# Self attentions of a decoder: transposed scores from a second product block in place of turned probabilities

## The reference

```python
xn = (x - mu) / jnp.sqrt(var + 1e-06) * ln_g + ln_b
qkv = xn @ w_qkv.T + b_qkv
q, k, v = (qkv[0], qkv[1], qkv[2])
scores = jnp.einsum('bhqd,bhkd->bhqk', q, k) * scale
scores = jnp.where(causal[None, None], scores, -jnp.inf)
probs = jax.nn.softmax(scores / TEMP, axis=-1)
gate = jnp.clip(jax.nn.sigmoid(xn @ w_ent.T + b_ent), 0.1, 2.0)[:, None, None, :, 0]
out = jnp.einsum('bhqk,bhkd->bhqd', probs * gate, v)
return (out @ w_out.T + b_out) * 0.1
```

```python
att = att1 - lam * att2
y = jnp.einsum('bhts,bhse->bhte', att, v)
y = y * jax.lax.rsqrt(jnp.mean(y * y, axis=-1, keepdims=True) + RMS_EPS) * subln_w
y = y * (1.0 - LAMBDA_INIT)
return y.transpose(0, 2, 1, 3).reshape(B, T, 2 * C) @ c_w.T
```

## Time and profile before

| | us |
|---|---|
| median of 3 runs | 6188.18 |
| lowest and highest | 6187.22, 6196.38 |
| the profiled execution | 6208.25 |
| its span | 6206.5 |

### The profile page before, as it was taken

The page is one execution under the profiler, slowest core; times in us unless marked ns, Lnnn a source line. Parts: engine busy times, 40 slices in busy tenths (PEclk is TensorE's granted clock), DMA queues, the critical chain, the costliest instruction groups (busy, mean ns, idle before and its releaser), DMA issues. The chain is left out here.

```text
span 6206.5 us, 84643 instructions
## 1 busy us (share of the span) xinstructions
PE 4731.2 (76%) x22582; PEld 3354.9 (54%) x22582; DVE 3437.1 (55%) x5067; ACT 2441.8 (39%) x3674; POOL 1999.7 (32%) x1091
## 2 busy tenths in 40 slices
PE   7999999999798866669878888888486444432698
PEld 6778778888544755348845555555274222221344
DVE  3444444444345422444556666664646999987444
ACT  2345555555222311123335555554123555540122
POOL 0055555555100000000036666664001555550000
PEclk7789999999799965687779999998677666655699
DMA  2100000000011312121111112110020000000011
GB/s 74 48 8 16 16 16 16 16 16 8 13 42 29 70 36 58 41 82 31 28 43 43 42 42 46 43 38 20 11 43 20 22 21 21 21 16 0 5 46 38
DMA packets 153375, 193.27 MB, mean 31 GB/s; under 512 B 91760, under 2 KB 136576, under 8 KB 152864
## 3 DMA queue, kind: packets, MB, share of 16 engines
q1 hardware_dynamic: 152992, 188.87, 12.5%
HBM read 134.07 MB, written 19.05 MB: 25 GB/s over the span
## 5 line engine op out<-in xcount | busy, mean ns | idle before, releaser
L1021 POOL TENSOR_TENSOR pexp_lo<-arena,pexp_hi 128x800 fp32r<-128x800 f32 x384 | 727.8, 1895 | 413.8 <-POOLq L1020 413.8
L976 POOL TENSOR_TENSOR pexp_lo<-arena,pexp_hi 128x800 fp32r<-128x800 f32 x384 | 628.4, 1636 | 515.6 <-POOLq L975 515.6
L1947 DVE TENSOR_REDUCE arena<-ps 128x1 f32<-128x482 f32 (+3 forms) x624 | 393.3, 657 | 404.1 <-DVEq L1925 388.9
L2092 DVE TENSOR_REDUCE arena<-ps 100x1 f32<-100x482 f32 (+1 forms) x768 | 476.6, 656 | 219.0 <-DVEq L2061 200.7
L1282 ACT ACTIVATE arena<-ps 128x800 f32<-128x800 f32 x384 | 322.3, 839 | 554.1 <-ACTq L1280 552.2
L1348 ACT ACTIVATE arena<-ps 128x800 f32<-128x800 f32 x384 | 321.7, 838 | 402.2 <-ACTq L1342 396.8
L2399 DVE MATCH_REPLACE8 arena<-arena 100x1444 f32<-100x1444 f32 x256 | 423.0, 1673 | 0.0
L3022 PE MATMUL ps<-kst,qs 96*100 96x482 f32 (+1 forms) x768 | 334.0, 436 | 116.4 <-PEq L2982 112.5
L1732 DVE TENSOR_REDUCE arena<-ps 100x8 f32<-100x800 f32 x160 | 158.7, 992 | 392.1 <-DVEq L1729 392.1
L3260 PE MATMUL ps<-arena,chunk 128*128 128x400 f32 x648 | 286.3, 524 | 72.6 <-PEq L3259 72.5
L2652 PE MATMUL ps<-w_const,arena 100*100 100x100 f32 x2560 | 311.2, 287 | 37.9 <-PEq L2648 37.9
(11 more groups left out here) (358 smaller groups left out, 11004.8 us busy)
## 6 DMA issues: line engine op xcount, KB each, us to landing
ctxT<-in_ctxT SPq DMA_DIRECT2D x64, 541.5 KB
ctxk<-in_ctx SPq DMA_DIRECT2D x48, 528.0 KB
kst<-mid SPq DMA_DIRECT2D x128, 180.5 KB, 3.1
heads_dram<-arena SPq DMA_DIRECT2D x20, 800.0 KB
chunk<-in_ff_chunks SPq DMA_DIRECT2D x77, 193.0 KB, 2.4
arena<-gate_dram SPq DMA_DIRECT2D x64, 200.0 KB, 3.1
kst<-xn SPq DMA_DIRECT2D x64, 180.5 KB, 2.9
q_rows<-heads_dram SPq DMA_DIRECT2D x36, 200.0 KB
```

The lines of the kernel that those rows point to most:

```text
L976: own(nc.gpsimd.tensor_tensor(pexp_lo[p % 3][:, :, :], pexp[p % 3], pexp_hi[p % 3][:, :, :], ALU.subtract))
L1021: own(nc.gpsimd.tensor_tensor(pexp2_lo[p % 3][:, :, :], pexp2[p % 3], pexp2_hi[p % 3][:, :, :], ALU.subtract))
L1947: peak = nc.vector.tensor_reduce(mparts[0:at.stop - at.start, m, c:c + 1], bank(k, z - a, at.stop - at.start), AX.X, ALU.max)
L2092: peak = nc.vector.tensor_reduce(mparts2[:, h, c:c + 1], bank(k, z - a, S), AX.X, ALU.max)
```

## The change

Queries and keys no longer go through DRAM. ACT copies the projected queries to `q_rows` and DVE the keys to `k_rows`, as plain f32 on 128 partitions. For each unit, DVE (keys, `k_diag`) and ACT (queries, `q_diag`) multiply them by `head_cols`, so that head j of each four stands alone in block j.

Scores are now f32 products over the 32 partitions of one group of four heads, three steps ahead of use, and they serve for the maxima alone. POOL sets the eight maxima on diagonals (`max_diag`). A second block of scores comes transposed: `lower` puts mask and minus maximum into banks 4 and 5 and `scoreT` adds keys times queries. The exponential reads these banks and writes `probsT` at once; turns, unread products, DVE's subtraction and ACT's two copies go. Values are products with 32 result rows, four heads below each other in bank 6. ACT copies the bank (`keep`); `gathered` picks out the sums, DVE inverts them, ACT widens them, `spread` turns them into bank 7, and DVE multiplies. The projection takes four products, over heads by rows. A unit is four batches in the third attention as well, once for each of the two attentions.

```diff
-                for k in range(8):
-                    turn(k, first and k == 0)
-                    if k < 6:
-                        scores(k + 2, par)
...
-                    if k > 0:
-                        values(k - 1, par)
...
+            def score(t, c):
...
+                r = slice(32 * (half + c), 32 * (half + c) + 32)
+                return mm(bank(2 * (t % 2) + c, GT, S), q_rows[sm][r, at], k_diag[par][r, :, own], start=not causal, stop=True)
...
+            def lower(t):
...
+                for c in range(2):
+                    if causal:
+                        mm(bank(4 + c, GT, S), id_bf, causalT_bf[:, :], start=True, stop=False)
+                    mm(bank(4 + c, GT, S), minus_ones[:, :], max_diag[t % 3][:, GT * c:GT * c + GT], start=not causal, stop=False)
...
+            def scoreT(t, c):
...
+                return mm(bank(4 + c, GT, S), k_rows[sm][r, at], q_diag[par][r, :, own], start=False, stop=True)
...
+            def values(t):
...
+                        ins = mm(ps[32 * j:32 * j + 32, 6, S * g:S * g + S], vaug[:, u // nsm % 2, at:at + 32],
+                                 probsT[:, t % 2, GT * c + S * j:GT * c + S * j + S], start=True, stop=True)
...
+            for t in range(8 * units):
+                more = t + 3 < 8 * units
+                if t > 0:
+                    pe.wait_ge(s.probsT_ready, 1)
...
+                    if causal:
+                        mask_scores(t + 3)
+                if t > 0:
+                    values(t - 1)
+                pe.wait_ge(s.diag_ready, 1)
...
+                lower(t)
...
+                if more:
+                    score(t + 3, 0)
+                scoreT(t, 0)
+                if more:
+                    score(t + 3, 1).then_inc(s.scores, 1)
+                scoreT(t, 1).then_inc(s.scoresT, 1)
+                if t % 2 == 0 and t >= 4:
+                    spread(wide)
+                if t % 2 == 1 and t >= 3:
+                    gathered(o_sb[(t // 2 - 1) % 2], "sum%d" % vw)
...
+            def project(G):
...
+                for g in range(4):
+                    ins = mm(bank(7), wo[:, 128 * g:128 * g + 128], y_rows[G % 2][:, g, :, :], start=g == 0, stop=g == 3)
```

More of the change, by code:

```diff
@@ L367, in build @@
     w_cross_at = place(w_cross)
-    packed = {k: w_cross if k in CROSS else sb("w_" + k, [128, dram[k].shape[1]]) for k in where}
+    packed = {k: w_cross if k in CROSS else sb("w_" + k, [128, dram[k].shape[1]]) for k in where if k != "masks"}
     def W(stage, name):
@@ L1116, in self_attention, with rows @@
             act.sem_inc(s.stage_act, -1)
-            def heads(to, m, g):
+            def rows(i, sm, g, key):
                 act.wait_ge(s.proj_full, 1)
                 act.sem_inc(s.proj_full, -1)
-                of = bs(bank(4 * (m % 2) + g))
+                to, of = (k_rows if key else q_rows)[sm][:, GT * g:GT * g + GT], bank(i % 8)
                 if cfg["bias"]:
-                    own(nc.scalar.activation(group(to, g), of, ACT.Identity, bias=W(SA[n], "bqk")[:, m:m + 1]))
+                    own(nc.scalar.activation(to, of, ACT.Identity, bias=W(SA[n], "bqk")[:, key:key + 1]))
@@ new lines, in self_attention @@
+            units = 4 * nsm
+            for i in range(4):
+                value_rows(0, i, VALUE_BANKS[i])
+            for t in range(8 * units):
+                u, k = divmod(t, 8)
+                kind, G, i = beside(nsm, t)
+                if kind == "values":
+                    value_rows(G, i, 7)
+                    act.sem_inc(s.proj_free, 1)
+                if squared_at(nsm, t) is not None:
+                    squared((u if k > 4 else u - 1) // nsm, squared_at(nsm, t))
+                if roots_at(nsm, t):
+                    roots()
+                if t % 2 == 0 and t >= 4:
+                    widen_sums()
+                if widened_at(nsm, t) is not None:
+                    widen_roots(widened_at(nsm, t))
+                act.wait_ge(s.scoresT, 1)
+                act.sem_inc(s.scoresT, -1)
+                nc.scalar.activation(probsT[:, t % 2, :].rearrange("p (c t) -> p c t", c=2), ps[0:S, 4:6, 0:GT], ACT.Exp,
+                                     scale=float(cfg["scale"])).then_inc(s.probsT_ready, 1)
+                if t % 2 == 0 and t > 0:
+                    keep(t // 2 - 1)
+                if 1 <= k <= 4 and u + 1 < units:
+                    diagonal(u + 1, k - 1)
@@ L1211, in cross_single @@
+            widen_sums()
+            keep(4 * units - 1)
+            if nsm == 2:
+                squared(NG - 1, 2)
+            widen_sums()
+            if nsm == 2:
+                squared(NG - 1, 3)
+                roots()
+                for i in range(4):
+                    widen_roots(i)
         def cross_single():
```

773 lines of the change are left out of this document (427 added, 346 removed).

## The result

The changed kernel takes **6244.6 us** (median of 20 runs, 6205.5 to 6277.9); the kernel before, run beside it, 6185.9 us (20 runs, 6135.1 to 6206.7). The ratio is 1.0099, 95% interval 1.0077 to 1.0121: slower by 1%, some 59 us. The forecast was 28 us slower. The profiled executions span 6239.2 us after and 6206.5 before, 33 us apart; the one of before is 22 us over its median of 20 runs, the one of after 4 us under its own.

A forecast was written before the change was run, and what follows sets the result against it. PE was taken to bound the loops. Loops +62, fronts -74, tails +27, clock start-up +12, start +1 gave +28 us on the 6188 median: 6216 us; own range 6170 to 6280, with rivals 6010 to 6465.

The forecast's parts named there:

- loops: The four attention loops: +62 us together (+18 twice, +40, -14), from steps of 5.85, 5.66 and 5.35 us.
- tails: What follows each attention loop: 75.5 us against 48.7, +27 us, with 15.5 each and 13 more in the third.
- fronts: What precedes each attention loop: 130.5 us against 204.4, -74 us, as DRAM, zeroing and waits go.
- all other stages: The program outside the attentions, some 5140 us, left alone; only +1 us at the start for masks and wo.
- five slots: Four score products a step, eight records: partial overlap, five slots of 0.335 us, 1.68 us in all.
- The first rival: Full overlap: all eight score records share 0.67 us, values fall to 0.67; -190 us, 6029 us; chance 0.24.
- The values' term: Eight f32 value products a step: 0.88 us, the middle between 0.35 side by side and 1.41 in a row.
- The exponential's leg: PE's wait each step from the scores' end through ACT's exponential to PE's next start: 1.30 us in all.
- The prediction's own last sentence: Wrong if POOL's product exceeds 2.5 us, a bank wait exceeds 0.3, or loops spend a third at the lower clock.
- The third rival: All loops granted 0.85, three steps in ten at the lower clock, 4.4 us more each: +206 us, 6422; chance 0.16.
- the second rival: No overlap of score or value products: +1.53 us a step, +239 us, 6455 us; chance 0.16.
- POOL: Its 100x800 product each step, nearest row 1.89 us, hides three steps ahead while a step is over 2.1 us.

The follow-up runs named there:

- e8: Changed kernel with all four score products of a step on the same 32 rows (first group's heads), none side by side; 6933.5 us.
- e9: Kernel before the change, without the four unread products it issues in each step; 6239.5 us, 1.0107 of the kernel before.
- e5: e1 plus three wide unread bf16 products (100 rows by 400 columns) in every step of all four attentions; 6099.5 us.
- e1: Changed kernel with the mask products and their wait for maxima moved ahead of the exponential's wait in the causal attentions; 6126.4 us.
- e3: Changed kernel with mask products ahead of the exponential's wait and value products put back behind the scores; 6026.3 us.
- e12: Changed kernel with masks ahead, values behind the scores, and two unread products in every step of all four attentions; 6018.4 us.

## Why the prediction was right and wrong

The sign, the range and, nearly, the profiled sum (+33 against +28) came out, but by luck, from errors that cancel: loops 35 us over their forecast and tails 39, fronts 10 and all other stages 59 under. By the medians the change costs 59 us, twice the forecast. Two steps failed. The scores were priced at five slots, 1.68 us, and take 0.87; and every term was priced at the full clock, with 0.95 or more granted in the loops, where 0.55 to 0.71 was granted.

- **The scores' term was mis-sized.** Five slots of 0.335, 1.68 us, were taken; the row shows two slots of about 0.43. The step that failed is the argument that a product's second record could share only with the next one's first. In the trace the four products do start and end in order, but all first records start, then all second ones. The first rival had the mechanism right (its price for the four was 0.67, a little low, and its own sum gives 6216 - 190 = 6026, not 6029).
- **The values' term** was 0.88, measured 0.48. Masks were 0.35, measured 0.44 (257.40 to 257.84); lowering 0.70, measured 0.83 (258.32 to 259.15), change of shape included. From the scores' start to the next step's first product the forecast had 1.68 + 1.30 = 2.98; measured are 1.12 (259.15 to 260.27) and 1.14 (256.26 to 257.40), 2.26. The whole step without side work: forecast 5.85 - 0.69 = 5.16, measured 4.01, so 1.15 a step too much, 179 us in 156 steps. The exponential's leg was a little short: from the last record's end (260.08) it was put at 0.15 + 0.84 + 0.14 = 1.13, and is 0.19 + 0.84 + 0.30 = 1.33.
- **The granted clock was the large miss.** Every duration in the sum was one of the full clock, and 0.95 or more was forecast for the loops; they got 0.55 to 0.71. The prediction's own last sentence named this case (a third of the time at the lower clock); it was some three quarters. By size: with the measured step the loops would be 813.6 + 62 - 179 = 697 us; they are 922.7, so the clock costs some 226 us. The third rival priced it at 206, and named both reasons: products on 32 rows, and a wait where the unread products stood. The runs over all rows and on one row group bear out the first (with the values as the rival left open), those that move the masks and values into the wait the second. Its price is near by luck: it took 0.85 in all loops and 4.4 us more for a step at the lower clock. Measured are 0.62 on average, three quarters of the time at the lower clock, and 6.12 - 4.01 = 2.1 us more for a step, since at the lower clock the wait is filled; 226 us is some 107 of 156 steps at that price, where the rival had 47.
- **Rivals one and three came together.** 6216 - 190 + 206 = 6232 would have been the forecast; the median is 6245. They had been weighed as alternatives, each with the other held still, and nothing kept them apart: narrow products came with a low clock side by side (0.55 to 0.71) and one after the other (e8, 0.51 to 0.53). So the second rival would have come with the third as well.
- **Fronts** -84 for -74: right, each within 5 us of its forecast (24.8, 16.9, 21.1, 57.5 for 29, 20, 25, 56.5).
- **Tails** +66 for +27: the list of products was right, but again priced at the full clock. The eight records of a projection in the first attention's loop, at the full clock, and of the last one in its tail:

```profile
263.02 2.85 PE L2820 MATMUL ps<-deviation,w_sa 128*128 128x400 f32 x8
...
286.46 5.67 PE L2820 MATMUL ps<-mid,w_sa 128*128 128x400 f32 x8 [1.26 <-PEq L2818]
```

 This alone is 2.8 of the 6.3 us by which the first tail exceeds its forecast.
- **Other stages** were held to be left alone. By the profile they are 58 us shorter:

```profile
263.50:2015.90 1752.40, 1630.93 (x7514) 1238.71 (x7514) 798.97 (x1348) 773.27 (x1069) 748.93 (x531) 0.93 0.07 17
...
293.80:2005.10 1711.30, 1598.95 (x7514) 1213.70 (x7514) 792.08 (x1348) 772.96 (x1069) 757.43 (x531) 0.94 0.08 19
```

 The first row is before, the second after: the cross attention behind the first self attention, same 7514 products, 41 us less. From the first attention's last exponential to the second's first the two traces of the old attention have 1800.8 (before) and 1795.4 (e9), the twelve of the new one 1750.8 to 1766.4; some 7 us of that are front and tail. The granted clock differs there: from 400 to 1000 us it is 0.95 before, from 430.3 to 1030.3 after it is 1.00. In one place of it PE waits 2.41 us before (to 725.91), and a good microsecond later its records take twice as long; the like wait of after (to 740.18) is 2.13 us, and all but two of the next records keep their length. Why the wait differs in a stage whose code is the same I did not find. Part of the prediction's hit by the profile is owed to this.
- **POOL** was no issue, as forecast: its product takes 1.52 us (L951) and ends no wait of the lowering in the steps shown. The sign that did come is the wait for bank 7 or what goes into it: PE stands still before spreads (L2804) for 3.9, 5.3, 10.9 and 5.4 us in the four attentions, up to 4.1 at a time in the third, where 0.3 had been named. That is small beside the clock.

## What to carry to other kernels

Packing narrow products side by side can shorten TensorE's chain by most of what the overlap promises (2.70 us to 0.87 here), and the loop can lose most of that to the granted clock (all but 43 of some 285 us); price such a loop at both clocks, and read the clock of each loop ahead of everything else in the profile after. Fill the exponential's wait with products that the steps need anyway (masks, values), which here took a change that cost 1% to one that gained 2.6%. Unread wide products paid less: 27 us in all four loops beside the masks (e5 against e1), where moving the values paid 100 (e3 against e1), and some 30 in the third attention once both moves were made; in a loop already near the full clock they are path (e12). And compare medians: one profiled execution of this kernel can be 20 to 35 us off its own.

## What was not expected of the hardware

Four f32 products on four row groups, two records each, run side by side: first records within 0.02 us, second ones within 0.02 us, 0.87 us for all against 2.70 in a row. Between two kernels that differ in the rows of four products, and the values that these rows hold, the granted clock of the first loop was 0.53 (32 rows, PE busy for 98.5% of it) and 0.99 (128 rows, 90%). At the lower clock a loop did not recover at once by being busy throughout (10.00 of 10 us at 0.50, for 30 us in one loop and some 70 in another). And beside an edit in one stage the clock of the next, whose products are the same, was another (0.95 and 1.00 in 600 us of it); why was not found.
